# Residuals, roots and two weight copies at the end of the opening round of a cross-attention and FFN kernel

## What is computed

```python
x = x + _L0_xattn_ref(_layernorm(x), ctx_1024, gamma, beta, w_q, w_kv, w_out, b_out, gate)
x = x + _L0_ffn_ref(_layernorm(x), w_gate, w_up, w_down)

# _L0_xattn_ref
xn = _layernorm(x) * gamma + beta
q = (xn @ w_q); k, v = split(context @ w_kv)          # 16 heads of 64
attn = softmax(q @ k.T / 8)
return ((attn @ v) @ w_out + b_out) * tanh(gate[0])

# _L0_ffn_ref: weights are integers times 1/127; 768 hidden columns
return (silu(x @ wg.T) * (x @ wu.T)) @ wd.T
```

## Time and profile before

| | |
|---|---|
| median of 3 runs | 293.44 us (293.13 to 293.5) |
| the profiled execution, its own time | 292.91 us |
| its span in the profile | 291.1 us |
| PE busy | 283.1 us, 97% of the span |
| DVE / ACT / POOL busy | 232.0 / 157.3 / 173.1 us |
| granted TensorE clock | full in all slices |
| length of a round | 28.28 us |

### The profile page before, as it was taken

How to read it: one execution, slowest core, us unless ns; L and a number is a source line. 1 busy time by engine, 2 the same in 40 slices (tenths; PEclk the granted TensorE clock), 3 DMA queues, 4 the chain that set the end, 5 groups by cost and what they waited for, 6 DMA issues and landing times.

```text
span 291.1 us, 6763 instructions
## 1 busy us (share of the span) xinstructions
PE 283.1 (97%) x2513; PEld 261.6 (90%) x2513; DVE 232.0 (80%) x611; ACT 157.3 (54%) x311; POOL 173.1 (59%) x199
## 2 busy tenths in 40 slices
PE   7999999999989999999999999999999999999995
PEld 7999978878969899989898989898989899988994
DVE  1598897788899789878986897789778987886773
ACT  3657875568057633853395349435933683156052
POOL 2653874369939681967296639654964587327133
PEclk9999999999999999999999999999999999999999
DMA  6995138522541013011201120112011201110002
GB/s 200 378 368 173 36 111 254 177 70 110 149 148 41 20 29 108 0 38 42 78 0 39 43 74 0 40 41 74 3 39 46 70 3 40 43 36 2 0 2 77
DMA packets 26668, 23.32 MB, mean 80 GB/s; under 512 B 12602, under 2 KB 24866, under 8 KB 26634
## 3 DMA queue, kind: packets, MB, share of 16 engines
q1 hardware_dynamic: 26634, 22.86, 25.1%
HBM read 15.87 MB, written 4.62 MB: 70 GB/s over the span
## 4 chain that ended last, share of the span: by engine, by line
PE 88%; DVE 6%; ACT 2%; issue 2%; POOL 0%; DVEq 0%
PE ps L927 13%; PE ps L869 10%; PE ps L828 6%; PE ps L836 6%; PE ps L832 6%; PE ps L752 5%; PE ps L996 5%; PE ps L997 5%; PE ps L1000 5%; PE ps L851 4%; PE ps L980 3%; PE ps L983 3%; PE ps L948 2%; PE ps L760 2%; PE ps L762 2%
## 5 line engine op out<-in xcount | busy, mean ns | idle before, releaser
L1251 POOL TENSOR_TENSOR probs<-probs,total 128x512 f32<-128x512 f32 x32 | 33.6, 1051 | 60.2 <-DVE total L1398 60.2
L1266 POOL TENSOR_TENSOR t_lo<-t_all,t_hi 128x1232 fp32r<-128x1232 f32 x16 | 45.7, 2858 | 3.0 <-ACT t_hi L1120 3.0
L1277 POOL TENSOR_TENSOR h_lo<-hid,h_hi 128x256 fp32r<-128x256 f32 x42 | 30.7, 737 | 22.2 <-ACT h_hi L1164 22.2
L1092 ACT COPY pt<-ps 128x512 f32<-128x512 f32 x32 | 19.1, 597 | 40.2 <-PE ps L851 40.2
L996 PE MATMUL ps<-wo_hi,o_hi 128*128 128x256 f32 x128 | 36.3, 284 | 0.0
L997 PE MATMUL ps<-wo_lo,o_hi 128*128 128x256 f32 x128 | 36.1, 282 | 0.0
L1000 PE MATMUL ps<-wo_hi,o_lo 128*128 128x256 f32 x128 | 35.9, 281 | 0.0
L1395 DVE TENSOR_REDUCE total<-probs 128x8 f32<-128x616 f32 x32 | 25.4, 793 | 7.8 <-ACT probs L1081 6.9
L1108 ACT CAST o_hi<-ps 128x512 fp32r<-128x512 f32 x32 | 17.2, 590 | 25.4 <-PE ps L869 25.4
L828 PE MATMUL ps<-t_hi,xn_hi 128*128 128x308 f32 x128 | 30.7, 321 | 0.0
L1381 DVE TENSOR_REDUCE top<-ps 128x4 f32<-128x308 f32 x64 | 28.4, 472 | 2.3 <-PE ps L836 2.3
(11 more groups left out here) (171 smaller groups left out, 836.4 us busy)
## 6 DMA issues: line engine op xcount, KB each, us to landing
x_ln<-in_x SPq DMA_DIRECT2D x8, 256.0 KB, 2.9
v_scratch<-v_out SPq DMA_DIRECT2D x4, 512.0 KB, 3.3
v_whole<-v_scratch SPq DMA_DIRECT2D x16, 128.0 KB
stream<-in_x SPq DMA_DIRECT2D x8, 256.0 KB, 2.9
x_rooms<-in_x SPq DMA_DIRECT2D x7, 256.0 KB, 7.4
out<-stream SPq DMA_DIRECT2D x7, 256.0 KB, 2.2
wk_raw<-in_L_xattn_w_kv SPq DMA_DIRECT2D x4, 256.0 KB, 4.6
wq_raw<-in_L_xattn_w_q SPq DMA_DIRECT2D x1, 1024.0 KB, 7.7
```

The costliest lines, as they stand in the source:

```text
L1251: nc.gpsimd.tensor_tensor(whole, whole, scale.to_broadcast([P, HR, HALVES, KEYS_WHOLE]), ALU.mult).then_inc(probs_done, 1)
L1266: nc.gpsimd.tensor_tensor(t_lo[:, :, cols], t_all[:, :, n, cols], t_hi[:, :, cols].bitcast(F32), ALU.subtract).then_inc(tlo_done, 1)
L1277: nc.gpsimd.tensor_tensor(h_lo[:, f, :], hid_of(b, f), h_hi[:, f, :].bitcast(F32), ALU.subtract).then_inc(hlo_done, 1)
```

## The change

In round 0:

- PE runs `O0 O1 D0 D1` in place of `O0 D0 O1 D1`.
- DVE runs `R0` ahead of `Z1` instead of behind it, `R1` behind `na6` instead of behind `na9` and the copy `Y0`, and the rest of the two roots by turns (`nb0 na7 nb1 na8 nb2 na9`).
- DVE no longer copies the fill of `D0` (`Y0`), and ACT no longer copies that of `D1` (`Y1`) at the end of round 0.

In round 1 a new stage `YF` on ACT, behind `X1`, makes both copies. As the banks are now held longer, PE waits for the first copy ahead of `XT` and for the second ahead of `G0`. SP's `WD` waits for both, and with it all that SP issues behind it.

In round 7 `DVE_END` goes the other way: all of `na0` to `na9` now stand ahead of `R1`, and `nb0` to `nb9` in one piece behind it.

```diff
-ACT_ORDER = "Ta C0 C1 E2 X1 O0 X t0 XH WO t1 E3 t2 h0 C2 Tb t3 h1 C3 h2 t4 E0 h3 O1 h4 t5 h5 E1".split()
+ACT_ORDER = "Ta C0 C1 E2 X1 YF O0 X t0 XH WO t1 E3 t2 h0 C2 Tb t3 h1 C3 h2 t4 E0 h3 O1 h4 t5 h5 E1".split()
-ACT_FIRST = "Ta C0 C1 E2 O0 X XH E3 C2 WO C3 Tb E0 O1 E1 Y1".split()
+ACT_FIRST = "Ta C0 C1 E2 O0 X XH E3 C2 WO C3 Tb E0 O1 E1".split()
-ACT_FILLS = "Y1".split()
-PE_FIRST = "T0 S2 T1 X1T S3 V0 XT G0 G1 T2 G2 G3 S0 T3 G4 G5 V1 S1 O0 D0 O1 D1".split()
-DVE_FIRST = "M2 LN Z2 X1 M3 O0 H0 Z3 H1 H2 H3 M0 H4 Z0 H5 O1 M1 Z1 R0 na0 na1 na2 na3 na4 na5 na6 na7 na8 na9 Y0 R1 nb0 nb1 nb2 nb3 nb4 nb5 nb6 nb7 nb8 nb9".split()
+ACT_FILLS = "Y0 Y1".split()
+PE_FIRST = "T0 S2 T1 X1T S3 V0 XT G0 G1 T2 G2 G3 S0 T3 G4 G5 V1 S1 O0 O1 D0 D1".split()
+DVE_FIRST = "M2 LN Z2 X1 M3 O0 H0 Z3 H1 H2 H3 M0 H4 Z0 H5 O1 M1 R0 Z1 na0 na1 na2 na3 na4 na5 na6 R1 nb0 na7 nb1 na8 nb2 na9 nb3 nb4 nb5 nb6 nb7 nb8 nb9".split()
...
-DVE_END = ("Z3.7 H0.7 H1.7 H2.7 H3.7 H4.7 O1.7 R0.7 na0.7 na1.7 na2.7 na3.7 na4.7 na5.7 na6.7 R1.7 nb0.7 na7.7 nb1.7 na8.7 "
-           "nb2.7 na9.7 nb3.7 nb4.7 nb5.7 nb6.7 nb7.7 nb8.7 nb9.7 lb xa xb H5.7 H0.8 H1.8 H2.8 Y0.7 Y1.7 H3.8 H4.8 H5.8 "
+DVE_END = ("Z3.7 H0.7 H1.7 H2.7 H3.7 H4.7 O1.7 R0.7 na0.7 na1.7 na2.7 na3.7 na4.7 na5.7 na6.7 na7.7 na8.7 na9.7 R1.7 nb0.7 nb1.7 "
+           "nb2.7 nb3.7 nb4.7 nb5.7 nb6.7 nb7.7 nb8.7 nb9.7 lb xa xb H5.7 H0.8 H1.8 H2.8 Y0.7 Y1.7 H3.8 H4.8 H5.8 "
...
# transpose_x, PE's XT
+                if isinstance(n, int) and n == 2:
+                    evacuated(pe, stand_in["D0"])
...
# gate_up, PE's G0
                 claim(b, f"G{f}")
+                if isinstance(b, int) and b == 1 and f == 0:
+                    evacuated(pe, stand_in["D1"])
...
# ACT's stages
-            for name in ACT_FILLS:
-                stages[name] = ("ffn", None)
-            stages["fill"] = lambda name: copy(copied_at[name]) if name in ACT_FILLS else None
+
+            def last_fills(b):
+                if b == 1:
+                    for name in ACT_FILLS:
+                        copy(copied_at[name])
+
+            stages["YF"] = ("ffn", last_fills)
```

## The result

The changed kernel took 292.68 us (median of 20 runs, 292.04 to 293.21), the kernel before 293.42 us (median of 20 runs beside it). The ratio is 0.9972 with a 95% interval of 0.9960 to 0.9983: 0.5 to 1.2 us less, 0.8 in the middle. That is a real gain, beyond the 0.59 us that I had called distinguishable in its middle but not at its lower end. 292.2 had been predicted, 1.25 us less.

A forecast was written before the change was run, and what follows sets the result against it. PE is busy 97% of the span, so only its waits for DVE's root steps, at X1T and xb, can pay. Gains 0.9 at T3 plus 0.35 in the tail make 1.25 us: 293.44 to 292.2, range 291.7 to 293.1.

The forecast's parts named there:

- the lock rival: Round 0: DVE root steps held to the end of POOL operations they meet; 0.85 us gained in all, chance 0.15.
- the prediction's own signs of being wrong: New wait of some tenths at T3 or h0, stretched na4 to na6, or round 7's R1 over 0.3 behind O1.
- the turns: Interleaving the two roots' steps on DVE costs 0.15 us in round 0; undoing it in the tail saves 0.15.
- The gain at X1T: Round 1, PE: R1 moves 1.2 us earlier, less 0.15 for interleaved root steps, so X1T comes 1.05 us earlier.
- a step is held by 0.25 at most, as the trace has it: Round 0 root steps beside P1: up to 0.25 us lost, 0.15 of it hidden by the x_ln limit.
- the long step: Tail, round 7: one DVE root step inside POOL's la took 0.41 against a median 0.16; its 0.25 us excess falls away.
- What arrives at T3: Round 1, PE: of the 1.05 us gained at X1T, 0.9 arrives at T3; bounds 0.5 and 1.1.
- The limit that I named, `x_ln`: Round 1: its load lands at 85.15 and holds LN, so Z2 starts only 0.9 us earlier, not 1.05.
- the landing may slip to 92.0 without loss: Round 1 down weights: landing expected at 91.4; beyond 92.0 each us late costs one us at T3.
- the rival "slower": Round 1: late down weights hold h0, P3 and T3; at 7.4 us DMA time 294.7 us; chance 0.04.
- The tail: Round 7: DVE_END back to one piece brings lb 0.4 us earlier, of which 0.35 counts; bounds 0 and 0.4.
- given back: T3, G0 or later takes most of DVE's gain back, 0.2 to 0.3 left of round 1; 293.0 to 293.2, chance 0.17.

The follow-up runs named there:

- the bare chain: A separate kernel: dependent one-column DVE steps beside single POOL operations, profiled once; beside the tensor_tensor a two-tensor step took 1.20 us in place of 0.16.

## Why the prediction was off in size

The 0.8 us lie within the stated range, and close to the 0.85 of the lock rival. That nearness is luck: as the distances show, the missing part has two causes, and one of them moves from execution to execution. Of the prediction's own signs of being wrong two appeared, the stretched `na4` and a new wait at `h0` and, in two profiles, at `T3`.

**Where DVE's own queue sets X1T.** Right, and the steps of its timeline with it. `R0` and `Z1` changed places at no cost to the roots, `R1` no longer waits for the copy or for `na7` to `na9`, and the turns cost about the 0.15 reckoned: from `nb0` to `LN1` 2.09 us against 1.91 before. The list of places where PE waits was short by one, the 0.66 us early in round 0, which the change does not touch.

**The gain at X1T, 1.05 predicted, 0.77 measured.** The step that failed is the one by which "a step is held by 0.25 at most, as the trace has it". `na4` was held 0.40 and `na5` 0.13. The lock rival was right on the mechanism: each step was held to the end of the POOL instruction that it met. Its price at `X1T` was about half of the 0.55 that it had (0.26 us, by the run with `Z1` first). It had put `R1` at 80.2; it came at 79.86 (80.09, less the 0.23 by which this execution was late at E1). `na4`, put at an end near 79.5, ended at 79.36, and `R1` starts 0.14 behind the start of `na6` without waiting for its end. I took 0.25 from the long step in `la`, which is a POOL tensor_scalar; `P1` is a tensor_tensor, and the bare chain shows that these two hold for different times. The Trainium skill, "SBUF — State Buffer", section "SBUF: two separate sides", has the loser blocked for the whole instruction: the trace and the bare chain agree for the tensor_tensor (held to within 0.02 us of its end) and not for the tensor_scalar. Of the 1.05 us, the version with `Z1` first has 1.03: the rest of the sum was right. (There `na5` is still held by 0.12, as it was by 0.10 in the kernel before.)

**What arrives at T3, 0.9 predicted, 0.63 in one profile and -0.08 in another.** The limit that I named, `x_ln`, did not bind, and would not have: where 1.04 was gained at `X1T` (`Z1` first, copies in round 0), 1.03 arrived at `T3`. The limit that I called safe did bind: "the landing may slip to 92.0 without loss". This is the term that cost most. With the copies in round 0, which take it away and leave the hold, the gain was 0.76 + 0.38 = 1.14 us, close to the 1.2 that the prediction gave for a held step. Two terms of it were mis-sized. The issue was put at 87.2; it was at 88.14, of which 0.2 is the later start of that execution, 0.3 the later `X1T`, and 0.5 stands between the end of the second copy (87.63) and the DMA, where the kernel before had 0.04 behind its last wait. And the landing was taken as 4.2 us from one row, which holds in the old place; in the new one it was 4.2 to 4.9. With both, the cover of 0.6 us was gone in all five profiles: B was above 11.19 by 0.12 to 0.85. The mechanism was the one of the rival "slower", in its place and its price (from 4.2 to 4.9 us of landing B grew by 0.71). It took back at most about what the opening had gained, and so did not make the kernel slower.

**The tail, 0.35 predicted, 0.37 measured.** Right in both of its parts: the turns and the long step are gone, and `R1` of round 7 starts where it did behind `O1`, 0.31 us after the start of its last matmul against 0.33 before.

**The covers.** The two copies on ACT cost nothing (0.64 us of idle time left before `O0`), and the waits of PE ahead of `XT` and `G0` neither: from `X1T` to `XT` 4.19 us before and after.

The sum by the measured terms is 0.77 + 0.37, less 0.12 to 0.85 at `T3`: 0.3 to 1.0 us, with the measured 0.8 in between. Two slips of the prediction's sums change nothing: "given back" with the tail comes to 292.8 and not 293.0, and the last case of "slower" to 294.8. Why the DMA is issued 0.5 us behind the second copy stays open: it was so in all five profiles with the copies in round 1.

## What to carry to other kernels

A duration that has to hold as cover should not be carried over from a row of the old place: the transfer took 4.2 us in every profile that issued it there with the same loads beside it, and 4.2 to 4.9 where it was moved to. There it is part of the path, and its scatter is the kernel's scatter. When a small chain on one engine is moved, look at what the neighbour engine runs beside it in the new place; here the order of two blocks of about the same length (`R0` and `Z1`) decided 0.26 us through what POOL ran beside the roots. And measure halves by distances inside the profile: 0.37 us of a 293 us kernel could not be told by its time, but was plain between two rows.

## What the runs showed of the hardware

- A DVE step with two SBUF tensors that meets a POOL tensor_tensor of 128x512 is held to its end (1.20 us in place of 0.16). Beside a POOL tensor_scalar of 128x256 that runs as long (1.22 us) it lost 0.08 us in the bare chain and 0.25 in the kernel's tail; beside a memset nothing. Operation, tensors read and columns differ together here, so which of them counts is not shown.
- The same arithmetic as tensor_scalar with two pointer scalars was held in none of the four profiles that have it (three of the kernel, one of the bare chain), but costs 0.05 us more a step (0.27 and 0.21 in place of 0.22 and 0.16).
- One DMA of 768 KB from SBUF to SBUF, with a load of 256 KB issued right behind it, landed in 4.2 us in five profiles that issued it in its old place and in 4.2 to 4.9 us in five that issued it about 4 us later; with a second load of 256 KB behind it, in 4.5 and 4.6 us.
